# Two score units of the fourth head group taken a stage earlier, and that group's maxima turned and sent one step sooner

## What is computed

```python
x = x + s * g                                   # end of layer 0
xn = _layernorm(x, axis=-1)
# attention of layer 1
k, q, v = proj(W_key), proj(W_query), proj(W_value)          # 8 x 16 heads x 512 x 16
scores = jnp.einsum('bhqd,bhkd->bhqk', q, k) * hd ** (-0.5)
scores = jnp.where(causal, scores, -jnp.inf)
weight = jax.nn.softmax(scores, axis=-1)
out = jnp.einsum('bhqk,bhkd->bhqd', weight, v)   # then W_proj
# gate of layer 1
w = jax.nn.softmax(-dists / t, axis=1)           # distances to 32 prototypes
topw, topi = jax.lax.top_k(w, 2)
out = sum over the two of topw * (A[topi] @ (B[topi] @ x) + bias[topi])
x = x + s * silu(out)
```

## Time and profile before

| | |
|---|---|
| median of 3 runs | 1019.94 us (1018.16 to 1020.38) |
| the profiled execution | 1019.23 us, its span in the trace 1017.4 us |
| TensorE busy | 965.3 us, 95% of the span |
| VectorE, ScalarE, GpSimd busy | 49%, 48%, 28% |
| mean granted TensorE clock | 0.993 |
| one batch of layer 1, middle of the kernel | about 75.9 us |

### The profile page before, as it was taken

The page is one execution under the profiler, slowest core; times in us unless marked ns, Lnnn a source line. Parts: engine busy times, 40 slices in busy tenths (PEclk is TensorE's granted clock), DMA queues, the critical chain, the costliest instruction groups (busy, mean ns, idle before and its releaser), DMA issues.

```text
span 1017.4 us, 21973 instructions
## 1 busy us (share of the span) xinstructions
PE 965.3 (95%) x7342; PEld 676.2 (66%) x7342; DVE 499.2 (49%) x1198; ACT 490.6 (48%) x1290; POOL 284.0 (28%) x295
## 2 busy tenths in 40 slices
PE   5999999999999998899999999999999999999985
PEld 2677777777778885555666766766766766766653
DVE  5013211231133455656567567567567567566541
ACT  2354444444443333365466466466466466464443
POOL 7111101120020004343444444434434434421000
PEclk9999999999999999898999999999999999999999
DMA  7511211123111035344244244244244244224110
GB/s 243 175 53 58 86 52 52 41 60 110 40 41 52 22 105 144 84 156 85 74 164 95 73 165 93 73 165 93 73 165 93 73 165 93 73 85 100 47 43 22
DMA packets 67978, 93.79 MB, mean 92 GB/s; under 512 B 11904, under 2 KB 54368, under 8 KB 67936
## 3 DMA queue, kind: packets, MB, share of 16 engines
q1 hardware_dynamic: 62992, 88.60, 30.8%
q10 hardware_dynamic: 4944, 4.66, 1.4%
HBM read 59.38 MB, written 33.59 MB: 91 GB/s over the span
## 4 chain that ended last, share of the span: by engine, by line
PE 33%; issue 11%; DVE 7%; POOL 6%; DMA 2%; ACT 1%; POOLq 0%; ACTq 0%; DVEq 0%; SPq 0%
PE PS L1166 5%; PE PS L1275 4%; DVE nm L2091 4%; PE PS L1219 3%; PE PS L1095 3%; PE PS L1190 2%; PE PS L1306 2%; PE PS L1116 2%; PE PS L1239 2%; PE PS L1237 2%; PE PS L1221 2%; POOL QB L834 2%; PE PS L1142 1%; POOL Q L826 1%; DMA Q<-nml 1%
## 5 line engine op out<-in xcount | busy, mean ns | idle before, releaser
L973 PE MATMUL PS<-arena 128*128 128x256 f32 x1024 | 313.9, 421 | 0.0
L1633 ACT ACTIVATE arena<-PS 128x512 f32<-128x512 f32 x256 | 151.6, 600 | 187.5 <-PE PS L1261 186.5
L2091 DVE TENSOR_REDUCE nm<-PS 128x1 f32<-128x512 f32 (+3 forms) x352 | 206.3, 635 | 60.6 <-PE PS L1223 60.5
L1481 ACT ACTIVATE arena<-PS 64x8 f32<-64x8 f32 x512 | 88.1, 172 | 193.3 <-PE PS L960 189.9
L960 PEld LDWEIGHTS PS<-arena 128*72 128x72 f32 x1024 | 129.2, 141 | 69.4 <-ACT arena L1481 6.5
L973 PEld LDWEIGHTS PS<-arena 128*128 128x128 f32 x1024 | 155.5, 192 | 0.0
L1841 DVE SCALAR_TENSOR_TENSOR arena<-arena 128x512 f32<-128x512 f32 x16 | 11.1, 694 | 227.0 <-ACT arena L1492 227.0
L960 PE MATMUL PS<-arena 128*72 128x8 f32 x1024 | 122.0, 191 | 0.0
L1237 PE MATMUL PS<-Q,K 128*128 128x128 bf16 x512 | 98.7, 221 | 11.9 <-DMA Q<-nml 10.6
L1239 PE MATMUL PS<-Q,K 98*128 98x384 bf16 (+2 forms) x384 | 97.1, 275 | 0.0
L1219 PE MATMUL PS<-K,Q 96*128 96x256 bf16 (+2 forms) x384 | 88.8, 275 | 4.6 <-DVE nm L2091 3.1
(11 more groups left out here) (254 smaller groups left out, 1489.3 us busy)
## 6 DMA issues: line engine op xcount, KB each, us to landing
qk_d<-QB SPq DMA_DIRECT2D x21, 512.0 KB, 2.9
Q<-qk_d SPq DMA_DIRECT2D x32, 192.0 KB, 3.7
K<-qk_d SPq DMA_DIRECT2D x31, 192.0 KB, 4.2
gt_d<-arena SPq DMA_DIRECT2D x16, 256.0 KB, 2.5
wx_d<-arena SPq DMA_DIRECT2D x16, 256.0 KB, 2.5
XT<-xt_d SPq DMA_DIRECT2D x8, 512.0 KB, 5.0
GT<-gt_d SPq DMA_DIRECT2D x8, 512.0 KB, 6.0
WX<-wx_d SPq DMA_DIRECT2D x8, 512.0 KB, 6.8
```

What stands on the lines that cost most here:

```text
L973: mm = pe.matmul(o, lhs, rhs, start=first, stop=last, skip_group_check=True)
L1481: s_.activation(HB[0:ST, nxt], PS[0:ST, 7, 0:B], ACT.Tanh).then_inc(c_h.sem, 1)
L1633: s_.activation(PR[:, g % 2, j, at:at + T], PS[:, bank, :], ACT.Exp).then_inc(t_e.sem, 1)
L2091: v_.tensor_reduce(nm[:, g, h:h + n, i], PS[:, u % 3, 0:n * (i + 1) * P].rearrange("p (n w) -> p n w", n=n), AX.X, ALU.max, negate=True).t ...
```

## The change

Units 0 and 1 of `scores(b, 3)`, with their maxima, leave step 0 of stage 2 and go to the last two steps of stage 1: on PE behind `turned(b, 1, 8)` and behind `turned(b, 1, 9)`, the latter ahead of `distance(b + 1)`; on DVE one between `remainder(b + 1, 2)` and `remainder(b + 1, 3)`, the other behind `keep_distance`. In stage 2 the transposition of the maxima of group 3 moves from step 6 to step 5. On ACT, `maxima_high(b, 3)`, `take_high(b, 3)` and `take_low(b, 3)` now all stand behind `exp` of step 5, and `expert_gate(b, 0)` moves from step 5 to step 6. `take_low` waits on ACT for `maxima_low` on DVE. Nothing is added or removed; the program of each engine only has another order.

```diff
             def stage(b, g, side, nxt, done=0):        # PE
                 for k in range(TQ):
                     turned(b, g, k)
                     if nxt is not None:
-                        for u in range(SU):
+                        for u in range(done, SU):
                             if STEP_OF[u] == k:
                                 scores(*nxt, u)
-                        if k == 6:
+                        if k == (5 if done else 6):
                             maxima_turn(*nxt)
                     run(side, k)
...
+                side.setdefault(8, []).append(lambda: scores(b, 3, 0))
+                side.setdefault(9, []).insert(0, lambda: scores(b, 3, 1))
                 stage(b, 1, side, (b, 2))
...
-                stage(b, 2, side, (b, 3))
+                stage(b, 2, side, (b, 3), 2)
...
             def stage2(b, more, more2):                # ACT
-                side = {1: [lambda: take_values(b, 1)], 5: [lambda: expert_gate(b, 0)],
-                        6: [lambda: maxima_high(b, 3), lambda: take_high(b, 3)], 7: [lambda: take_low(b, 3)], 8: [],
+                side = {1: [lambda: take_values(b, 1)], 6: [lambda: expert_gate(b, 0)],
+                        5: [lambda: maxima_high(b, 3), lambda: take_high(b, 3), lambda: take_low(b, 3)], 8: [],
                         9: [lambda: expert_gate(b, 1)]}
...
             def stage(side, nxt, done=0):              # DVE
                 for u in range(SU + 1):
-                    if nxt is not None and u < SU:
+                    if nxt is not None and done <= u < SU:
                         maxima(*nxt, u)
...
                 if more:
                     remainder(b + 1, 2)
+                    maxima(b, 3, 0)
                     remainder(b + 1, 3)
                     keep_distance(b + 1)
+                    maxima(b, 3, 1)
+                else:
+                    maxima(b, 3, 0)
+                    maxima(b, 3, 1)
...
-                stage(side, (b, 3))
+                stage(side, (b, 3), 2)
```

More of the change, by code:

```diff
@@ L1312, in run, with stage @@
                     step()
-            def stage(b, g, side, nxt):
+            def stage(b, g, side, nxt, done=0):
                 for k in range(TQ):
@@ L2124, in add_rows, with stage @@
                                             op0=ALU.mult, op1=ALU.add).then_inc(z_v.sem, 1)
-            def stage(side, nxt):
+            def stage(side, nxt, done=0):
                 for u in range(SU + 1):
-                    if nxt is not None and u < SU:
+                    if nxt is not None and done <= u < SU:
                         maxima(*nxt, u)
```

## The result

The changed kernel took 1034.37 us (median of four runs, 1029.61 to 1038.05) against 1019.05 us for the kernel before beside it: ratio 1.0147, 95% interval 1.0103 to 1.0192. It is 15 us slower, where the forecast was 1015.4. The profiled execution took 1034.66, with a span of 1032.9. From here on the edit shifts ACT's and DVE's lines by two (L2074 of before is L2076 of after; L1546, L1588, L2068 and L2091 are L1548, L1590, L2070 and L2093); PE's up to L1314 and POOL's keep their numbers.

A forecast was written before the change was run, and what follows sets the result against it. PE, busy 95% of the span, was taken to bound the kernel. Gains of 4.05 (batch 0), 6 x 0 and 0.50 (batch 7) made 4.5 us, from the median 1015.4 us; range 1009.2 to 1019.2.

The forecast's parts named there:

- the sum: Whole kernel: 4.05 us from batch 0, 0 from batches 1 to 6, 0.50 from batch 7, 4.5 in all.
- the last rival: Stage 3, batches 0 to 5: L788 ahead of the split's second cast or L2074 holds it 2.36 us; 1029.6, chance 0.10.
- The steps for batch 0: Border of stages 2 and 3: unit 4 starts 5.10 behind stage 2, not 9.15, clock 1.00; gain 4.05 us.
- batch 7: End of stage 1: two score units move into PE's idle time of 1.34 us; gain 0.50 us.
- batches 1 to 6: Border of stages 2 and 3: the memset still holds the cast, unit 4 stays 5.10 behind stage 2; gain 0.
- the cast that grows to 1.66: Cast L2068 on DVE starts earlier but ends when it did, behind the memset; about 1.6 us.
- The 2.88 of the clock in batch 0: Stage 3: the shorter stall keeps the clock at 2.4 GHz, winning 2.88 us of the 4.05.
- 1.17 of stall: Start of stage 3 in batch 0: the earlier transfer removes 1.17 us of PE's stall, part of the 4.05.
- the clock is not won: Rival on batch 0: low row lands with the last loads, or clock falls elsewhere; 1018.3 us, chance 0.12.
- The wait for the low row: PE's total wait for the low row of the maxima falls from 10.6 us to about 4 or less.
- new waiting for the maxima: PE's score matmuls (L1219) wait anew for DVE's maxima (L2091), about 1 us in each of batches 0 to 6.
- The cast did not slip ahead of the memset: Rival for batches 1 to 6: cast starts before the memset and takes 0.23 us; 1009.3 us, chance 0.12.

The follow-up runs named there:

- e8: The changed kernel with the third part of the split made by a reduction reading one SBUF input instead of two: 1017.19 us, ratio 0.9985.
- e1: The changed kernel with one more wait on POOL, so L788 starts only when the expert weights are split in all three parts: 1016.45 us, ratio 0.9987.
- e3: The kernel before with POOL's memset of stage 3 (L826), and so L788, waiting for the whole split: 1017.86 us, ratio 0.9987.
- e5: The changed kernel with the old transposition step and old ACT order, so only the two score units move: 1017.41 us, ratio 0.9974.
- e4: The kernel before with ACT's L1546 one slot earlier, at the end of stage 2, so that L788 comes earlier: 1032.3 us, ratio 1.0151.
- e6: The kernel before with the transposition at step 5 and ACT's new order, score units where they were: 1035.5 us, ratio 1.0157.
- e7: The changed kernel with five filling matmuls on an unused bank in front of unit 3 in stage 3: 1031.6 us, ratio 1.0103.

## Why the prediction was wrong

**The step that failed** is a cost that the sum put at nothing: the third part of the split (L2074) was taken to keep its 0.29 us with L788 starting ahead of it. It was held for L788's whole run, 2.46 us, in five batches, and unit 4 came 2.18 later in each. The mechanism was written down, but only in the last rival: L788 would come 0.35 earlier, and "The page's other half (two SBUF inputs contend too) would do the same by way of L2074, which now starts 0.04 behind L788". The trace has 0.33 and 0.03. The rule is that of the Trainium skill's GPSIMD Engine Reference (Specifications, the row on SBUF interfaces), and e8 bears it out for this pair, 2.46 us against 0.29. The prediction gave the case 0.10 and left it out of the range, with the remark "No row here shows a two-input instruction held, and none excludes it". But with L788 computed to come 0.04 ahead, the whole case hung on that rule alone; and of the rule's two halves the trace had already shown one, the held cast.

The remark overlooks rows of the kernel before that bear on the other half, and they speak for the forecast (batch 2, POOL and DVE):

```profile
618.80 1.75 POOL L816 TENSOR_TENSOR near<-near,halves 128x8 f32<-128x8 f32 x1 [9.16 <-DVE near L2039]
618.97 0.29 DVE L2042 TENSOR_TENSOR wm<-iota,topf 128x128 f32<-128x128 f32 x1
...
622.26 0.29 DVE L2064 TENSOR_TENSOR wm<-wm,hit 128x128 f32<-128x128 f32 x1
```

L2042 and L2064 both read two SBUF inputs. One starts 0.17 behind POOL's L816, the other 0.38 behind the start of the memset L826, and neither is held. So a low chance had something in its favour. What neither row shows is a GpSimd instruction that reads as much as L788: L816 reads 8 columns where L788 reads 1024, and the memset reads none. An outcome worth 15 us that depends on such an unseen pair belongs at an end of the range, whatever its chance.

**Its price.** 6 x 2.36 - 4.5 gave 1029.6; measured 1034.4. Three terms differ. It was five batches and not six, as in batch 0 the third part escapes by 0.15 us. A hold costs 2.18, not 2.36. And the clock was not in it: a stall of about 2.5 us in five batches gave 1.8 each, although batch 0 of before had shown such a fall behind 2.02 us of idling. With these the sum is 5 x (2.18 + 1.8) - 4.5 = 15.4, and the two profiled executions differ by 1034.66 - 1019.23 = 15.4. That it comes out so closely is in part luck: 1.8 is an average over three batches, and the 4.5 holds for the profiled execution of before, whose clock fell in batch 0, and not for the medians.

**The gain was half of what was forecast, for another reason.** The steps for batch 0 (5.10, clock 1.00), batch 7 and batches 1 to 6 (gain 0 behind the memset) hold, and so does the cast that grows to 1.66. But e1, the change without the collision, gained 2.3 us in the medians and not 4.5. The 2.88 of the clock in batch 0 is the term mis-sized: it was in the one profiled execution of before, and other traces have it smaller, not at all, or in another place. Windows of e3, which idles 1.42 there, of e5, which idles 1.59, and of batch 7 in e1, behind 1.10 of idling:

```profile
468.00:474.00 6.00, 6.00 (x68) 3.51 (x69) 4.82 (x11) 3.26 (x6) 4.15 (x2) 1.00 0.59 127
...
467.60:470.80 3.20, 3.20 (x20) 1.31 (x21) 3.10 (x8) 1.63 (x2) 1.37 (x2) 0.50 1.00 209
471.00:474.00 3.00, 3.00 (x41) 1.54 (x33) 1.18 (x3) 1.07 (x2) 1.04 (x1) 1.00 0.02 3
...
969.00:975.00 6.00, 5.57 (x40) 2.05 (x41) 0.75 (x2) 0.60 (x1) 0.00 (x0) 0.50 0.30 90
```

Over the runs of the kernel before beside e1 to e4 the mean granted clock is 0.990 to 0.995 and the time goes with it (1016.97 to 1017.85 at 0.995); e1 at 0.995 and 0.996 has 1014.8 to 1016.19. At an equal clock that is about 1.8 less, and the forecast's 1.17 of stall and 0.50 of batch 7 make 1.67. The rival "the clock is not won" (1018.3, chance 0.12) was the better forecast of this part.

**What holds otherwise.** The wait for the low row, forecast at 4 or less, is 5.1, as batches 0, 2 and 4 keep some tenths. "About 1 us" of new waiting for the maxima in each batch is too much even without the hold: e1 has 5.8 us over the span where before had 3.1, some 0.4 more a batch. The cast did not slip ahead of the memset.

## What to carry to other kernels

An edit that lets one engine go earlier moves the start of every GpSimd instruction released by it: list which VectorE instruction with two SBUF inputs, or which cast, now starts behind the start of a long one, to a few hundredths of a microsecond, and price that case with the stall and the clock that the stall costs. If the chain behind VectorE's instruction is critical and GpSimd's is not, one wait that puts GpSimd's behind it is worth more than the edit itself (1.0147 turned to 0.9906 here). If two late causes cover each other, removing either alone shows nothing. And a fall of the clock seen in one profiled execution is not a gain to count in full.

## What the hardware showed that was not expected

- **The hold has a fixed end, not a rate.** A two-input VectorE instruction that starts 0.03 behind GpSimd's 2.35 us one takes 2.46, one that starts 0.17 behind it takes 2.34, and one that starts 0.15 ahead takes its 0.29 (after, e4, batch 0 of after). The price jumps from nothing to all of it within 0.18 us.
- **It depends on the pair.** While L788 (GpSimd, two inputs of 1024 columns, 2.35 us) runs, a one-input reduction (0.29, e8) and an operation with one input from SBUF and one from PSUM (0.68, L2086 in batch 0) are not held. While the memset L826, which only writes, runs, a multiplication (0.28) and an addition with two SBUF inputs (0.29, both e4) are not held, and the cast from fp32 to bf16 is (1.17 in before). While L816 (GpSimd, two inputs of 8 columns, 1.75 us) runs, L2042 with two SBUF inputs is not held (0.29). The row of the Trainium skill's GPSIMD Engine Reference (Specifications, SBUF interfaces) sets no condition on GpSimd's instruction; L788 agrees with it, the memset and L816 do not, so by these rows that side matters. That it is the amount that GpSimd reads is a guess. Whether L788 would hold the cast was not tried: no row has them together.
- **A stall of 2.4 to 2.8 us takes the clock down often, but not each time.** In after it fell to 0.50 behind all five such stalls, for 3 us or more in batch 1 and over 6 in batch 3; in e6 behind four of five (behind the 2.44 of batch 3 it stays at 1.00 from 705 to 712); in e4 behind two of five stalls of 1.8 to 2.1. Five small matmuls in the stall kept it at 1.00 in all five batches (e7).
